# Second cross attention of a two-layer decoder: key projections taken two chunks at a time

## The reference, cut to what matters

```
q = (x @ Wq).reshape(b, n, H, DH)                 # n = 1024 queries, H = 16 heads, DH = 64
k = (context @ Wk * SCALE).reshape(b, m, H, DH)   # m = 6404 keys, DH = 64
v = (context @ Wv).reshape(b, m, H, DH)
scores = jnp.einsum('bihd,bjhd->bhij', q, k)
attn = jax.nn.softmax(scores, axis=-1)
out = jnp.einsum('bhij,bjhd->bihd', attn, v)
return out.reshape(b, n, H * DH) @ Wo + bo
```

## Time and profile before

| | us |
|---|---|
| median of 3 runs (5543.52 to 5548.84) | 5547.38 |
| the profiled execution | 5513.86 |
| its span | 5512.1 |
| PE busy | 4651.9 (84%) |
| DVE busy | 3773.2 (68%) |
| ACT busy | 2570.0 (47%) |
| the rough K projection L954, 128x512, 384 matmul instructions | 228.1 |
| the K copies L1062, L1064, L1097, 64x512, 192 each | 114.2, 113.7, 120.2 |
| the K rest L1148, 64x512, 192 | 133.4 |

### The profile page before, as it was taken

One profiled execution on the slowest core, in us unless ns is written; L12 is line 12 of the kernel. 1 busy time (PEld: TensorE's weight loads), 2 busy tenths in 40 slices (PEclk: granted clock), 3 DMA queues, 4 the chain that ended last, 5 costly groups with the idle time before them and its releaser, 6 DMA issues. The chain is left out here.

```text
span 5512.1 us, 68466 instructions
## 1 busy us (share of the span) xinstructions
PE 4651.9 (84%) x21823; PEld 2160.6 (39%) x21823; DVE 3773.2 (68%) x4226; ACT 2570.0 (47%) x4400; POOL 866.4 (16%) x798
## 2 busy tenths in 40 slices
PE   6898677767677777769969999999999999999993
PEld 2333343434343343423334444444444444444441
DVE  3666464737364655536648888888988888888865
ACT  1454463636363545515524555545555545545550
POOL 0000453625253544400010000000000000000000
PEclk6887798989898898968869999999999999999996
DMA  0000000000000000000000000000000000000000
GB/s 16 3 2 0 32 13 10 1 21 1 21 1 21 1 16 5 1 10 1 1 27 2 2 3 3 3 3 1 4 2 3 3 3 3 1 4 1 1 1 8
DMA packets 18039, 35.07 MB, mean 6 GB/s; under 512 B 3418, under 2 KB 12250, under 8 KB 16746
## 3 DMA queue, kind: packets, MB, share of 16 engines
q1 hardware_dynamic: 17642, 30.22, 1.7%
HBM read 29.69 MB, written 0.52 MB: 5 GB/s over the span
## 5 line engine op out<-in xcount | busy, mean ns | idle before, releaser
L1089 ACT ACTIVATE xat_p_full<-xat_sc 128x512 f32<-128x512 f32 (+1 forms) x1632 | 881.4, 593 | 677.4 <-PE xat_sc L1019 666.9
L1151 DVE TENSOR_REDUCE xat_part<-xat_ring 128x2 f32<-128x1024 f32 (+1 forms) x832 | 971.8, 1183 | 92.1 <-PE xat_ring L973 77.1
L1182 DVE TENSOR_TENSOR xat_p_sum<-xat_p_sum,xat_p_full 128x1024 f32<-128x1024 f32 x768 | 936.7, 1220 | 47.9 <-ACT xat_p_full L1089 40.4
L999 PE MATMUL xat_acc<-xat_p_full,xat_v 128*64 128x512 f32 (+1 forms) x3264 | 881.7, 618 | 2.5 <-ACT xat_o_raw L1094 2.5
L1018 PE MATMUL xat_sc<-xat_q_hh,xat_k_hl 128*128 128x512 f32 (+1 forms) x1632 | 785.6, 481 | 4.8 <-ACT xat_p_full L1089 4.7
L1019 PE MATMUL xat_sc<-xat_q_lm,xat_k_h 128*128 128x512 f32 (+1 forms) x1632 | 645.3, 395 | 0.0
L1018 PEld LDWEIGHTS xat_sc<-xat_q_hh,xat_k_hl 128*128 128x128 f32 (+1 forms) x1632 | 304.0, 186 | 497.9 <-ACT xat_p_full L1089 363.6
L1435 PE MATMUL loc_pr<-loc_w_qkv,loc_xs 128*128 128x512 f32 x576 | 364.8, 767 | 101.5 <-DVE loc_cosd L1703 56.0
L971 PE MATMUL xat_ring<-xat_k_hl,xat_q_hh 64*128 64x512 f32 (+1 forms) x832 | 387.6, 483 | 63.7 <-DVE xat_k_hl L1148 19.5
L1848 POOL PARTITION_ALL_REDUCE quant_top<-quant_part x5 | 1.8, 358 | 2681.9 <-DVE quant_part L1871 2681.9
L973 PE MATMUL xat_ring<-xat_k_up,xat_q_hh 64*128 64x512 f32 (+1 forms) x832 | 388.4, 484 | 0.0
(11 more groups left out here) (393 smaller groups left out, 7236.8 us busy)
## 6 DMA issues: line engine op xcount, KB each, us to landing
loc_w_qkv<-in_L_ffn_w SPq DMA_DIRECT2D x6, 1536.0 KB, 7.1
loc_w_o<-in_L_ffn_wo SPq DMA_DIRECT2D x6, 512.0 KB, 3.3
xat_ctxT<-in_ctxT SPq DMA_DIRECT2D x12, 256.0 KB, 2.7
xat_w_qk<-in_L_xattn_wqk SPq DMA_DIRECT2D x16, 128.0 KB, 2.4
loc_w<-in_L_ffn_w SPq DMA_DIRECT2D x6, 341.0 KB, 3.0
loc_w<-in_L_ffn_w SPq DMA_DIRECT2D x6, 192.0 KB, 2.3
loc_rope<-in_rope SPq DMA_DIRECT2D x1, 1024.0 KB
xat_w_o<-in_L_xattn_wo SPq DMA_DIRECT2D x16, 64.0 KB, 1.8
```

Of the source, the lines that this page charges most:

```text
L999: last = pe.matmul(acc[h * GROUP:(h + 1) * GROUP, :], v[0:size, t, e * GROUP:(e + 1) * GROUP], p_full[0:size, t % 3, cols(h)], start=(t == ...
L1089: act.activation(p_full[0:size, j % 3, cols(h)], sc[0:size, n % 3, :], ACT.Exp, scale=GROUP ** -0.5).then_inc(S["exp_done"], 1)
L1151: ins = dve.tensor_reduce(part[:, 2 * t:2 * t + 2, c], ring[:, b, :, 0:chunks[c][1]], AX.X, ALU.max)
L1182: dve.tensor_tensor(p_sum[:, e, :], first_in, p_full[:, (j - 1) % 3, :], ALU.add)\
```

## The change

Chunks are taken in couples. The order of chunks is now 9, 10, 11, 12, 0, ... 8, and the couples are (9,10), (11,12), (0,1), (2,3), (4,5), (6,7) and (8). A K item is one couple: the first chunk is projected with 64 weight columns into rows 0 to 63 of the slot, the second into rows 64 to 127 of the same bank. ACT makes the same two copies for each chunk, so four for a couple, and signals once behind the fourth. DVE makes the same subtraction for each chunk, two for a couple, and the slot is freed behind the second. The K items are in steps 2, 4, 9, 17, 25, 33 and 37. `k_up` has six buffers in place of three, and four chunks in place of two have storage of their own. In `first`, a couple is in every second step. The order of the engines' lists, the M items and their steps, and the other items stay; which chunk an M item belongs to follows the new order, so that the four of the 260-wide chunk move from steps 7 to 10 to steps 14 to 16.

```diff
-    OWN = NCH - 2
+    OWN = NCH - 4
...
+    couples = [order[n:n + 2] for n in range(0, NCH, 2)]
+    NK = len(couples)
...
-                for n, c in enumerate(order):
-                    steps[(2, 4)[n] if c >= OWN else PER * c + 5][pre] += [("K", c, 0)]
+                for n, couple in enumerate(couples):
+                    steps[2 + 2 * n if couple[0] >= OWN else PER * couple[-1] + 5][pre] += [("K", n, 0)]
...
                 for n, c in enumerate(order):
-                    steps[n + 1][pre] += [("K", c, 0)]
+                    if n % 2 == 0:
+                        steps[n + 1][pre] += [("K", n // 2, 0)]
...
-        k_up = s.sb("k_up", [P, 3, BANK], F32R)
+        k_up = s.sb("k_up", [P, 6, BANK], F32R)
...
# TensorE
-                        lo, width = chunks[c]
-                        if part is first:
-                            pe.wait_ge(S["ctx_loaded"], 16 * (order.index(c) + 1))
-                        last = pe.matmul(ring[:, b, 0, 0:width], w_qk[:, nxt, P:2 * P], ctxT[:, lo:lo + width],
-                                         start=True, stop=True)
+                        for m, chunk in enumerate(couples[c]):
+                            lo, width = chunks[chunk]
+                            if part is first:
+                                pe.wait_ge(S["ctx_loaded"], 16 * (order.index(chunk) + 1))
+                            half = slice(m * GROUP, (m + 1) * GROUP)
+                            last = pe.matmul(ring[half, b, 0, 0:width], w_qk[:, nxt, P:P + GROUP],
+                                             ctxT[:, lo:lo + width], start=True, stop=True, skip_group_check=True)
...
# ScalarE
-                            act.activation(k_up[GROUP:P, order.index(c) % 3, 0:width], ring[GROUP:P, b, 0, 0:width],
-                                           ACT.Copy)
-                            act.activation(k_hl[0:GROUP, lo:lo + width], ring[0:GROUP, b, 0, 0:width], ACT.Copy)\
-                               .then_inc(S["hi_done"], 1)
-                            copies.append((lo, width, hi))
+                            for m, chunk in enumerate(couples[c]):
+                                lo, width = chunks[chunk]
+                                lo = key_at(nxt, lo)
+                                half = slice(m * GROUP, (m + 1) * GROUP)
+                                act.activation(k_up[GROUP:P, (2 * c + m) % 6, 0:width], ring[half, b, 0, 0:width],
+                                               ACT.Copy)
+                                last = act.activation(k_hl[0:GROUP, lo:lo + width], ring[half, b, 0, 0:width],
+                                                      ACT.Copy)
+                                copies.append((lo, width, hi))
+                            last.then_inc(S["hi_done"], 1)
...
# VectorE
-                            lo, width = chunks[c]
-                            key = slice(key_at(nxt, lo), key_at(nxt, lo) + width)
-                            ins = dve.tensor_tensor(k_hl[GROUP:P, key], ring[GROUP:P, b, 0, 0:width],
-                                                    k_up[GROUP:P, order.index(c) % 3, 0:width], ALU.subtract)
+                            for m, chunk in enumerate(couples[c]):
+                                lo, width = chunks[chunk]
+                                lo = key_at(nxt, lo)
+                                high = k_up[GROUP:P, (2 * c + m) % 6, 0:width] if m else k_hl[0:GROUP, lo:lo + width]
+                                ins = dve.tensor_tensor(k_hl[GROUP:P, lo:lo + width],
+                                                        ring[m * GROUP:(m + 1) * GROUP, b, 0, 0:width], high,
+                                                        ALU.subtract)
```

More of the change, by code:

```diff
@@ L969, in item @@
                         if t == 0:
-                            pe.wait_ge(S["hi_done"], at_.heads(NCH + 1, NCH + 1 + n + 2))
+                            pe.wait_ge(S["hi_done"], at_.heads(NK + 1, NK + 1 + n // 2 + 2))
                         pe.matmul(ring[:, b, 0, 0:width], q_hh[0:GROUP, nxt, 2 * t * P:(2 * t + 1) * P],
@@ L973, in item @@
                         last = pe.matmul(ring[:, b, 1, 0:width], q_hh[GROUP:P, nxt, (2 * t + 1) * P:(2 * t + 2) * P],
-                                         k_up[GROUP:P, n % 3, 0:width], start=True, stop=True)
+                                         k_up[GROUP:P, n % 6, 0:width], start=True, stop=True)
                     elif kind == "T":
@@ L1059, in body @@
                             hi += 1
-                            lo, width = chunks[c]
-                            lo = key_at(nxt, lo)
-                            act.activation(k_up[GROUP:P, order.index(c) % 3, 0:width], ring[GROUP:P, b, 0, 0:width],
-                                           ACT.Copy)
-                            act.activation(k_hl[0:GROUP, lo:lo + width], ring[0:GROUP, b, 0, 0:width], ACT.Copy)\
-                               .then_inc(S["hi_done"], 1)
-                            copies.append((lo, width, hi))
+                            for m, chunk in enumerate(couples[c]):
[8 more added lines that the diff above has]
+                            last.then_inc(S["hi_done"], 1)
                         elif kind == "V":
@@ L1095, in body @@
                     for lo, width, n in copies:
-                        act.wait_ge(S["hi_done"], at_.heads(NCH + 1, NCH + 1 + n))
+                        act.wait_ge(S["hi_done"], at_.heads(NK + 1, NK + 1 + n))
                         act.activation(k_h1[0:GROUP, lo:lo + width], k_hl[0:GROUP, lo:lo + width], ACT.Copy)\
@@ L1137, in body @@
                             hi += 1
-                            dve.wait_ge(S["hi_done"], at_.heads(NCH + 1, NCH + 1 + hi))
+                            dve.wait_ge(S["hi_done"], at_.heads(NK + 1, NK + 1 + hi))
                         else:
```

## The result

The changed kernel takes 5567.2 us (median of 15 runs, 5552.7 to 5581.6) against 5529.5 (15 runs of the kernel before beside it). The ratio is 1.006, with a 95% interval of 1.0046 to 1.0074: slower by 25 to 41 us. Forecast were 5587, which is +40 from a median of 5547.4; more runs brought that median down to 5529.5, so that +38 came. The profiled execution took 5573.8 after and 5513.9 before, 60 more. Of these, 18 lie ahead of this stage, where the two kernels are the same (its first item starts at 2815.4 and at 2797.2), and 42 in it. The comparison therefore goes head by head.

The account below looks back on a forecast made before the run. PE was taken as the bound, DVE close behind and tied to it by short buffers. Seven odd heads at +3.7, seven even at +2.5, head 0 +1.2 and the part before -5 gave +40 on 5547.4: 5587, range 5548 to 5625.

Parts of the forecast that it names:

- PE work: K items on PE: a couple at 1.01 in place of 1.72, 3.8 us less per head, bounds 0 and 4.7.
- Rival A: Column halves of a couple don't overlap: the 3.8 us per head are not saved, 57 more, 5644; chance 0.05.
- The lump: Four copies, two subtractions hold a couple's slot until 5.08, 3.14 before; odd heads' V waits 1.50 each, 6.0 per head.
- The start of the head: Steps 2 to 6: new stalls, odd 0.5 + 2.35 + 1.0 + 1.2, even 2.2 + 1.0 + 1.6.
- Even heads: M items wait behind couples: 2.7 at step 9, 0.38 at three others, later reduction waits; sum 5.5, net +2.5 per head.
- Part before head 0: Waits for DVE in every step; couples in every second step save 0.8 in each of six pairs: -5, bounds -10 and 0.
- Head 0: Has no U, Y and V; saved work, new stalls and old stalls gone come to about +1.2.
- Rival B: PE is the bound and the slot's longer stay is hidden, deciding at slot free 3.58: gain 62, 5485; chance 0.09.
- Rival C: New stalls of steps 2 to 6 replace old ones, 2.6 less per head: +4, 5551; 0.13 with -11 to +11.

Follow-up runs that it names:

- e10: Changed kernel without column halves: a couple's chunks projected one after the other with 128 weight columns, each into its own bank; ratio to the kernel before 1.0177.
- e2: Changed kernel with ACT signalling behind each chunk's two copies in place of behind the couple's fourth copy; ratio to the kernel before 0.9919.
- e5: Changed kernel with the first M item of step 4 of every filling head issuing its matmuls six times, useless PE work; ratio to the kernel before 1.0035.
- e3: Changed kernel with the second and third couple at steps 9 and 13 in place of 4 and 9, later ones shifted; ratio to the kernel before 0.9978.
- e1: Changed kernel with each V item of odd heads one step later; ratio to the kernel before 1.0071.
- e9: Changed kernel with V later, a signal for each chunk and early couples later, but without column halves; ratio to the kernel before 1.001.

## Why the prediction was right, by its own steps

**PE work.** From a couple to the next scores it takes 0.95 (4101.61 to 4102.56), 1.01 said. But the prediction set this distance against the 0.86 of a K item, which is a difference of two step lengths. Measured that way a couple costs 0.86 too, and 5 x 0.86 + 0.43 = 4.7 us are saved per head where 3.8 was said: the bound that it gave for a couple that costs no more than one chunk. Rival A is out by the trace, and e10 shows its price: +65 us, 57 said.

**The lump.** DVE starts 3.50 behind the couple (3.61 said), the slot is free at 4.95 (5.08). The V item waits 1.36 four times in odd heads (1.50). e2 shows that this is the cause: with the same work and the slot free 0.7 earlier, the wait is 0.68.

**The start of the head.** Step 3 waits 0.30 (0.5), the second M of step 4 2.27 (2.35), V of step 6 0.90 (1.0), M of step 6 0.91 (1.2); even 1.97, 0.90, 1.34 (2.2, 1.0, 1.6). Where the clock is low behind step 4, V of step 6 waits less than 0.90, since PE comes to it later.

**Even heads.** The M of step 9 waits 1.84 and its V item 0.58 (2.7 together said). The M items of steps 18, 26 and 34 start 4.95 behind their couple, when the slot is free; that makes their step 0.30 longer (0.38 said), though the trace records no idle time for it. The other later waits come to 1.0 (0.28 and 0.75; 1.7 said). A likely reason, not tested: the narrow M items, which now lie in steps 14 to 16, give DVE 0.5 each, and I had counted that move at nothing.

**What was left out: the clock.** I gave the stage the granted 1.00 that the rows showed and never asked what a longer stall would do to it. The 21 falls cost at most half of the 65 us of added half-clock time, 32 us, and e5, which removes the 13 of step 4, shows 14 (0.0025 of 5530) by the ratios and 19 by the heads for 48 us less at half clock. An estimate from these 19 of 48: the 65 us cost about 26 of the 38 us that the heads lost.

**How the sum comes out.** For an odd head the work and the waits as measured give -4.7 + 9.8 - 3.45 = +1.7, and the mean is +3.64, which leaves 2.0 for the clock; half of the odd heads' added time at half clock is 2.2 each. For an even one they give -4.7 + 7.7 + 0.9 - 4.0 = -0.1 and the mean is +1.8 (+2.5 said), which leaves 1.9 of at most 2.4. That +3.7 was said and +3.64 came is in part luck: the work saved was put 0.9 too low and the waits 1.2 too high, and together they stood in for the clock, which was counted at nothing. The way of the change and the wait behind the lump were no luck, as e2 shows.

**Part before head 0.** -5 was said, 0 came: from its first Q item to the first scores of head 0 it takes 115 us before and after, and a pair of steps takes 16.7 for 16.6, where 0.8 less was said. In every second step, where the K item is gone, DVE waits for PE instead, which runs the V item at low clock ahead of the M items; the first row is DVE in a step with a couple, the second in one without:

```profile
2848.43 0.69 DVE L1158 TENSOR_TENSOR xat_k_hl<-xat_ring,xat_k_hl 64x512 fp32r<-64x512 f32 x1 [3.38 <-ACT xat_k_hl L1071]
...
2855.30 4.62 DVE L1162 TENSOR_REDUCE xat_part<-xat_ring 128x2 f32<-128x1024 f32 x4 [2.29 <-PE xat_ring L978]
```

I had let the M items start at once there, and this term of the sum failed. The mean granted clock over this part is 0.55 where it is 0.69 before, which the sum had not either; how the 5 us divide between the two is open. With a signal for each chunk (e2) the part takes 111. Head 0 is about 3 us longer where 1.2 was said.

**Rival B** decides, as it said, by when the slot is free; e2 moves that from 4.95 to about 4.26, still above 3.58, and already gains 0.8%. So the threshold was put too low: at 4.26 the waits left are less than the 4.7 us of work saved. **Rival C** is out: the new waits of steps 3 to 6 come to 4.4 us in an odd head where 5.05 was counted, 0.7 less and not 2.6, and e3 shows that what the start of the head costs, clock included, is 3.1 to 3.8 us per head.

Two slips in the prediction's text change nothing in its sum: in an even head DVE's 133.6 is 16 us below PE's 149.5, which is 11% and not 16%, and rival C's time is 5551 where the range names it 5548.

The Trainium skill, TensorEngine Tiling (Array Packing), PSUM Bottleneck, has the mechanism, and this trace agrees: the projection got twice as fast (0.86 for two chunks in place of 1.72), while emptying its slot takes 3.9 us behind it (4102.68 to 4106.56). What costs time here is less the emptying itself, which is the same work as before, than that the slot is held for both chunks. The Trainium skill's TensorE: Matmul & The Clock Gate, Part 1, says that the low clock is the default and activity releases it; the trace agrees in so far as 0.50 is granted behind the idle time of 2.27 and not behind that of 1.12 in e5, but the length of one idle time does not decide it here (below).

## What to carry to other kernels

Joining two items saves work on the engine that makes them and holds their buffer for both evacuations; read off how long the buffer stays and which item wants it next before counting the saving. Signal each part of a joined item as soon as it is done: here that alone was worth 1.4%. Lay the joined items where the next user of the buffer is far. When a change makes a stall of TensorE longer, ask what the clock does behind it: here stalls of 1.97 to 2.28 us in 13 of 14 heads were followed by half clock, and the work behind them took up to 2.0 us longer. And measure an item's price before and after by the same distance, best from a step with it and a step without it.

## What the runs showed of the hardware that was not expected

- Behind the stalls of 1.97 to 2.28 us at step 4, in heads where PE is otherwise busy, the granted clock fell to 0.50 in 13 of 14 heads, for some 3.6 us on the mean (75 us in 21 falls); behind 1.12 (e5) and 1.01 (e2) in the same place it never did. No stall length decides it alone. In e1 the same 1.98 was without a fall in four of seven even heads. In e10 a stall of 1.79 at step 4 was followed by one in 1 of 14 heads, and in e2 a stall of 1.15 at step 9 in 3 of 7. The kernel before has three falls in heads 1 to 15, one of them behind waits of 1.35 and 1.07 in step 5 and 6 that all its heads have.
- Matmuls that keep PE busy with useless work made the kernel faster (e5).
- Repeats of one M item follow each other at 0.23 us, where an M item among others takes 0.43.
- Two float32 projections of 512 columns side by side in column halves cost 0.86, as much as one alone with 128 weight columns; one behind the other they cost 1.71 (e9, e10).
